# Conditioned low-rank layer and tanh recurrence on one core: the prologue's loads and products in another order, three quarters of W2 in whole rows

## Chip, core and metric

The kernel runs on one NeuronCore of a Trainium2 chip. The metric is the device time of one launch in microseconds (us), the median of the runs shown.

## What is computed

The input x has 4 batches of 512 time steps with 256 channels, all float32. A first layer adds a correction to x. Its weights are partly made from a condition vector per batch:

```
c = layernorm(cond) * gamma + beta
w = gelu(c @ W1 + bias1) @ W2 + bias2          # W2: 256 x 8192
a1, b1, a2, b2 = four parts of w, each 256 x 8 per batch
mid = gelu(x @ base_down + (x @ a2) @ b2^T)
x = x + mid @ base_up^T + (mid @ b1) @ a1^T    # the kernel adds x twice: this sum and the last one
```

A second layer is a recurrence over the 512 steps, `h = tanh(x_t @ Wx + b + h @ Wh)`, and the output is x plus all the h.

## The kernel before

**The stages.** The prologue makes the four factors A2, B2, B1 and A1 from W2, applies them to the first 64 time steps, and prepares the first 16 inputs of the recurrence. Then 512 recurrence steps run one after the other (`over_pairs(recurrence)`, L976). In each step TensorE does 24 small bf16 products on split weights (L881), ScalarE does two tanh (L462), and VectorE makes the residues (L544, L548). Work for later time steps is put between the steps from a table written by hand (`fill_product`, `turn_more_rows` L853, `turn_rows` L864, `input_product`). The order of everything is written out by hand for each engine. Engines meet through semaphores only, and each engine runs its list in order.

**The loads.** SyncE issues all large loads in one list (L307 to L319): the first 64 rows of x per batch, W1, base_down, then A2 and B2 of W2, Wh, base_up, B1, Wx, A1, the other 64 rows of x's first tile, and three more tiles of x. `load_w2` (L301) splits each of the four parts of W2 into four transfers of 128 rows by 1024 columns (4 KB of each row): column half c outside, row half k inside. W2's partition axis holds the rows, k is which 128 of the 256 rows. ScalarE issues six small loads (L393 to L398), the last two being b_rnn and bias2.

**TensorE's list in the prologue** (L651 to L779, L948 to L976): warm-up products on zeros (`keep_busy`, L646 to L649, each a 128x256 bf16 product that nothing reads), the transposed condition (L655), 12 more on zeros, the transposed first rows of x (L669), bias1 (L718), the transposed normalized condition (L722), base_down (L675) and W1 (L732). Then, for each of the four parts, `bias_product` (L661) starts a bank with bias2, and `w_products` (L678) adds, for one column half c, the products of both row halves k. That is 16 instructions on L682: two k, four column strips e, and two passes of a float32 product.

**What VectorE does with them.** `keep_rank` (L521) waits until a column half of a part is complete, multiplies by a mask (L524, wmul) and sums over the rank (L527, fac). `spread` (L530, instruction at L531) lays the factor out as a block matrix, for B2 (b2d) and A1 (a1d) alone. Its list is: A2 halves 0 and 1, a copy, B2 half 0 and its spread, u0 (L558), B2 half 1 and its spread, B1 halves 0 and 1, v0, then for each half n of A1 its rank sum, its spread and `make_x2` (L535). `turn_factor` (L688, instruction at L691) turns A2 and B1 on TensorE. L755 is x @ a2, L767 adds b2d to mid, L698 is base_up, L708 adds a1d, L785 and L790 start the first inputs of the recurrence.

**GpSimd** makes constants, then splits b, Wh and Wx into bf16 parts (L361 to L388). The split of Wh and of Wx takes five instructions each and starts when the load has landed. A memset of h_ring (L389) follows.

Of the kernel before, what the change touches and what calls it, by code (L numbers as in the profile page):

```python
# [32 lines left out]
def adaptive_lowrank_then_recurrence(nc, x, cond, base_up, base_down, ln_gamma, ln_beta, W1, bias1, W2,  # L33
# [24 lines left out]
    with ExitStack() as ctx:  # L58
# [16 lines left out]
        x_sb = sb("x_sb", [P, B, NTT, D])  # L75
# [69 lines left out]
        ld_x = [sem(f"ld_x{n}") for n in range(NTT)]  # L145
        ld_x_more = sem("ld_x_more")
# [84 lines left out]
        def hpre(m):  # L231
            return (bank[7], bank[3])[m][:, D + B * m:D + B * (m + 1)]
# [62 lines left out]
        def _(sp):  # L295
            w2v = W2.rearrange("(k p) (j n) -> k p j n", p=P, j=NTYPE)

            def load_x(n):
                sp.dma_start(x_sb[:, :, n], x[:, P * n:P * (n + 1)].rearrange("b p d -> p b d")).then_inc(ld_x[n], 16)
# [92 lines left out]
        def _(act):  # L392
# [52 lines left out]
            def fill_more_rows(h):  # L445
                act.wait_ge(rows_psum, h + 1)
                nc.scalar.copy(xT[:, :, 2 * h:2 * h + 2, T0:P],
                               more_rows_out(h).rearrange("p (k b t) -> p k b t", k=K2, b=2)).then_inc(rows_moved, 1)
# [40 lines left out]
        def _(dve):  # L489
            steps = [0]  # L490

            def then_wait(ins):
# [23 lines left out]
                                  bank[2][:, 0:K2 * B]).then_inc(cT_ready, 1)  # L516
# [126 lines left out]
        def _(pe):  # L643
            zeros_h = zeros[:].bitcast(BF16)
            pe.wait_ge(pool_step, 1)
            def keep_busy(n, spare=0):  # L646
                for _ in range(n):
                    nc.tensor.matmul(bank[spare][:, D:2 * D], zeros_h[:, 0:P], zeros_h[:, 0:D], start=True, stop=True,  # L648
                                     skip_group_check=True)  # L649

            keep_busy(WARM)  # L651
# [6 lines left out]
            keep_busy(12)  # L658

            def bias_product(j, c):  # L660
                nc.tensor.matmul(wbank(j, c), quadrant[:].rearrange("e i q -> e (i q)"),  # L661
                                 bias2_sb[:, j, c], start=True, stop=False, skip_group_check=True)
# [338 lines left out]
```

## Time and profile before

| | us |
|---|---|
| median of 3 runs (526.58 to 527.30) | 526.85 |
| the profiled execution, device time | 527.65 |
| its span, first to last instruction | 525.9 |
| TensorE busy (matmuls) | 505.6 |
| VectorE busy | 291.8 |
| ScalarE busy | 175.2 |
| GpSimd busy | 22.2 |
| start of the first product of recurrence step 0 after x is ready (L790) | 37.57 |

The profile's times count from the first instruction. PE is TensorE's matmuls and PEld its weight loads, DVE VectorE, ACT ScalarE, POOL GpSimd, SP SyncE, and a q behind an engine means its queue. L682 is line 682 of the kernel. The DMA engines are nearly fully busy in the first 35 us (slices of 13 us move 292, 401 and 213 GB/s) and nearly idle after that. "128x256 f32" is partitions by elements. In the chain that ended last, each piece is followed back from the last instruction to what released it, so its pieces add up to the elapsed time. A piece of PE ends where the next one's result begins, some hundredths of a us after the start that the timeline shows.

### The profile page before, as it was taken

To read this page: it belongs to the slowest core of one execution; us is meant where nothing else is said; L and a number is where in the kernel's file an instruction comes from. 1 tells how busy PE (TensorE), PEld (TensorE's weight loads), DVE (VectorE), ACT (ScalarE), POOL (GpSimd) and SP (SyncE) were. 2 spreads that over 40 slices of the span, in tenths; PEclk is the share of its full clock that TensorE was granted. 3 is DMA by queue.
4 is the path that set the end of the run, shared out by engine and by line. 5 is a ranking of instruction groups with operands and counts; after the bars stand their busy time and mean duration, and the time that the engine had idled before them with its cause. 6 is when DMAs were issued, how large, how long until landed. Compare 5 with 4: busy or idle time off the path is not lost.

```text
span 525.9 us, 33134 instructions
## 1 busy us (share of the span) xinstructions
PE 505.6 (96%) x14756; PEld 471.9 (90%) x14756; DVE 291.8 (55%) x2272; ACT 175.2 (33%) x1158; POOL 22.2 (4%) x35
## 2 busy tenths in 40 slices
PE   9999999999999999999999999999999999998885
PEld 6569999999999999999999999999999999998884
DVE  2535565565556556555655555555655655565553
ACT  3103333333333333333333333333333333333322
POOL 7350000000000000000000000000000000000000
PEclk9999999999999999999999999999999999999999
DMA  8970000000000000000000000000000000000000
GB/s 292 401 213 4 4 14 4 4 14 4 14 5 14 6 7 11 4 14 4 15 4 14 4 6 14 4 14 4 14 4 5 14 4 15 4 14 3 14 6 11
DMA packets 8114, 16.05 MB, mean 31 GB/s; under 512 B 500, under 2 KB 5924, under 8 KB 7972
## 3 DMA queue, kind: packets, MB, share of 16 engines
q1 hardware_dynamic: 7904, 13.90, 7.8%
q8 instruction: 115, 1.88, 1.5%
q14 instruction: 27, 0.22, 0.1%
q10 hardware_dynamic: 68, 0.05, 0.0%
HBM read 11.85 MB, written 2.10 MB: 27 GB/s over the span
## 4 chain that ended last, share of the span: by engine, by line
PE 94%; ACT 3%; issue 1%; DVE 1%; DVEq 0%; POOL 0%; POOLq 0%
PE bank L881 64%; PE bank L801 7%; PE bank L845 4%; PE bank L826 3%; ACT h_ring L462 3%; PE bank L850 2%; PE bank L840 2%; PE bank L821 2%; PE bank L831 2%; PE bank L648 2%; PE bank L682 2%; PE bank L810 1%; PE bank L661 1%; PE bank L785 1%; PE bank L869 1%
## 5 line engine op out<-in xcount | busy, mean ns | idle before, releaser
L881 PE MATMUL bank<-h_ring,whp 128*128 128x52 bf16 x6132 | 243.3, 186 | 13.2 <-ACT h_ring L462 13.2
L544 DVE TENSOR_TENSOR r_ring<-h_ring 128x4 f32<-128x4 f32 x1022 | 136.6, 164 | 205.7 <-ACT h_ring L462 203.2
L462 ACT ACTIVATE h_ring<-bank 128x4 f32<-128x4 f32 x1024 | 142.1, 174 | 320.3 <-PE bank L881 312.5
L881 PE MATMUL bank<-r_ring,whp 128*128 128x52 bf16 x4096 | 220.5, 185 | 0.0
L881 PEld LDWEIGHTS bank<-h_ring,whp 128*128 128x128 bf16 x6132 | 187.9, 96 | 34.2 <-ACT h_ring L462 25.8
L881 PEld LDWEIGHTS bank<-r_ring,whp 128*128 128x128 bf16 x4096 | 174.6, 96 | 0.0
L881 PE MATMUL bank<-l_ring,whp 128*128 128x52 bf16 (+1 forms) x2048 | 157.4, 178 | 0.0
L548 DVE TENSOR_TENSOR l_ring<-r_ring 128x4 bf16<-128x4 f32 x1024 | 136.2, 162 | 0.0
L881 PEld LDWEIGHTS bank<-l_ring,whp 128*128 128x128 bf16 x2048 | 122.5, 96 | 0.0
L801 PE MATMUL bank<-xp,wxp 128*128 128x32 bf16 x1488 | 63.0, 176 | 0.0
L801 PEld LDWEIGHTS bank<-xp,wxp 128*128 128x128 bf16 x1488 | 50.5, 96 | 0.0
L845 PE MATMUL bank<-mid,upT 128*128 128x128 f32 x120 | 28.1, 316 | 0.0
L826 PE MATMUL bank<-xT,down_sb 128*128 128x128 f32 x112 | 26.2, 316 | 0.0
L785 PE MATMUL bank<-ones,b3h 128*128 128x32 bf16 x128 | 22.4, 176 | 0.0
L845 PEld LDWEIGHTS bank<-mid,upT 128*128 128x128 f32 x120 | 17.9, 188 | 0.0
L826 PEld LDWEIGHTS bank<-xT,down_sb 128*128 128x128 f32 x112 | 16.7, 188 | 0.0
L592 DVE TENSOR_TENSOR y_sb<-x2T,h_ring 128x64 f32<-128x64 f32 x64 | 15.4, 283 | 0.6 <-ACT h_ring L462 0.6
L840 PE MATMUL bank<-mid,b1T 128*128 128x128 f32 x60 | 14.0, 316 | 0.0
L850 PE MATMUL bank<-v_sb,a1d 128*128 128x128 f32 x60 | 14.0, 316 | 0.0
L821 PE MATMUL bank<-xT,a2T 128*128 128x128 f32 x56 | 13.1, 316 | 0.0
L831 PE MATMUL bank<-u_sb,b2d 128*128 128x128 f32 x56 | 13.1, 316 | 0.0
L648 PE MATMUL bank<-zeros 128*128 128x256 bf16 x72 | 12.0, 319 | 1.0 <-POOL zeros L338 1.0
(123 smaller groups left out, 240.4 us busy)
## 6 DMA issues: line engine op xcount, KB each, us to landing
w_sb<-in_L_cond_W SPq DMA_DIRECT2D x16, 512.0 KB, 11.5
out<-o_sb SPq DMA_DIRECT2D x16, 128.0 KB
x_sb<-in_x SPq DMA_DIRECT2D x3, 512.0 KB, 15.2
x_sb<-in_x SPq DMA_DIRECT2D x2, 256.0 KB, 9.6
w_sb<-in_L_cond_W SPq DMA_DIRECT2D x1, 256.0 KB, 3.6
down_sb<-in_L_cond_base_down SPq DMA_DIRECT2D x1, 256.0 KB, 5.0
wh_sb<-in_L_cond_Wh SPq DMA_DIRECT2D x1, 256.0 KB, 11.1
up_sb<-in_L_cond_base_up SPq DMA_DIRECT2D x1, 256.0 KB, 11.3
```

The source lines that it names most:

```text
L462: nc.scalar.activation(h_ring[:, m, slot(pair, s), 0:B], zt, ACT.Tanh).then_inc(h_ready, 1)
L544: nc.vector.tensor_tensor(r_ring[:, k, q, 0:B], state_before(pair, s, k)[:, 0:B], state_hi_before(pair, s, k)[:, 0:B], ALU.subtract).then_ ...
L548: nc.vector.tensor_tensor(l_ring[:, k, q, 0:B], r_ring[:, k, q, 0:B], r_hi[:, k, q, 0:B], ALU.subtract).then_inc(l_ready, 1)
L785: nc.tensor.matmul(zbank(p, q, m)[:, 0:TC // 2], b3h[:, P * m:P * (m + 1)], ones[:], start=True, stop=False, skip_group_check=True)
L801: nc.tensor.matmul(zb, wxp[w][:, k, P * m:P * (m + 1)], rhs, start=False, stop=False, skip_group_check=True)
L821: ins = nc.tensor.matmul(columns(fill_out(tile, 0)), a2T[:, k].rearrange("p e q -> p (e q)"), xT[:, k, :, t0:t0 + BL], start=(k == 0), sto ...
L826: nc.tensor.matmul(columns(fill_out(tile, 1 + c)), down_sb[:, k, P * c:P * (c + 1)], xT[:, k, :, t0:t0 + BL], start=(k == 0), stop=False)
L831: nc.tensor.matmul(columns(fill_out(tile, 1 + c)), b2d[:, P * c:P * (c + 1)], u_sb[:], start=False, stop=True).then_inc(fmid_psum, 1)
L840: ins = nc.tensor.matmul(columns(fill_out(tile, 0)), b1T[:, k].rearrange("p e q -> p (e q)"), rhs, start=(k == 0), stop=(k == K2 - 1))
L845: nc.tensor.matmul(columns(fill_out(tile, 1 + c)), upT[:, k, P * c:P * (c + 1)], rhs, start=(k == 0), stop=False)
L850: nc.tensor.matmul(columns(fill_out(tile, 1 + c)), a1d[:, P * c:P * (c + 1)], v_sb[:], start=False, stop=True).then_inc(fup_psum, 1)
L881: return nc.tensor.matmul(zbank(p, q, m)[:, col0:col0 + n], whp[part][:, k, P * m:P * (m + 1)], rhs[:, 0:n], start=False, stop=stop, skip_ ...
```

## The change

- W1 is loaded first and with two adjacent rows per partition (`(p k)` in place of `(k p)`), then base_down and Wh. The condition is turned in the same order. The first rows of x come behind A2, in a tile of their own (xa_sb) with two adjacent time steps per partition. Their transposes are four of 128x128 in place of eight of 64x64. The other 64 rows of the first tile (xb_sb) are loaded and turned the same way. Wx is loaded ahead of B1.
- `load_w2` loads A2, B2 and B1 in two transfers each of 128 whole rows of 8 KB (1 MB), and A1 in four as before.
- On ScalarE bias2 is loaded ahead of b_rnn, and the Gelu of the condition comes ahead of the copies of the turned x.
- On TensorE `w_half_products` does one column half c for one row half k. For A2, B2 and B1 both column halves of k = 0 come first, then both of k = 1, so both halves of a part are complete within one k. All bias products come earlier, into banks that two parts share (B1 and A1 in the upper 256 columns). The x work comes behind A2's products. B1's products come behind base_up, with nine products on zeros behind each k.
- In the last stretch three quarters of A1 come ahead of its first use and one quarter behind it. Some first products of step 0 come earlier.

The diff, cut to its core:

```diff
-        PLACE = {A2: 0, B2: 2, B1: 0, A1: 2}
+        PLACE = {A2: (0, 0), B2: (2, 0), B1: (0, HC), A1: (2, HC)}
         def wbank(j, c):
-            return bank[PLACE[j] + c][:, 0:HC]
+            first, col = PLACE[j]
+            return bank[first + c][:, col:col + HC]
...
             def load_w2(j):
+                if j != A1:
+                    for k in range(K2):
+                        sp.dma_start(w2_sb[:, k, j], w2v[k, :, j]).then_inc(ld_w2[j][0][k], 16)
+                    return
                 for c in range(2):
                     for k in range(K2):
                         sp.dma_start(w2_sb[:, k, j, 2 * CH * c:2 * CH * (c + 1)],
                                      w2v[k, :, j, 2 * CH * c:2 * CH * (c + 1)]).then_inc(ld_w2[j][c][k], 16)
-            sp.dma_start(x_sb[0:T0, :, 0], x[:, 0:T0].rearrange("b p d -> p b d")).then_inc(ld_x[0], 16)
-            sp.dma_start(w1_sb[:], W1.rearrange("(k p) n -> p k n", p=P)).then_inc(ld_w1, 16)
+            sp.dma_start(w1_sb[:], W1.rearrange("(p k) n -> p k n", p=P)).then_inc(ld_w1, 16)
             sp.dma_start(down_sb[:], base_down.rearrange("(k p) n -> p k n", p=P)).then_inc(ld_down, 16)
+            sp.dma_start(wh_sb[:], Wh.rearrange("(k p) n -> p k n", p=P)).then_inc(ld_wh, 16)
             load_w2(A2)
+            sp.dma_start(xa_sb[:].rearrange("p r d -> p (r d)"),
+                         x[:, 0:T0].rearrange("b (q r) d -> b q (r d)", r=2)).then_inc(ld_xa, 16)
             load_w2(B2)
-            sp.dma_start(wh_sb[:], Wh.rearrange("(k p) n -> p k n", p=P)).then_inc(ld_wh, 16)
             sp.dma_start(up_sb[:], base_up.rearrange("(k p) n -> p k n", p=P)).then_inc(ld_up, 16)
+            sp.dma_start(wx_sb[:], Wx.rearrange("(k p) n -> p k n", p=P)).then_inc(ld_wx, 16)
             load_w2(B1)
-            sp.dma_start(wx_sb[:], Wx.rearrange("(k p) n -> p k n", p=P)).then_inc(ld_wx, 16)
             load_w2(A1)
-            sp.dma_start(x_sb[T0:P, :, 0], x[:, T0:P].rearrange("b p d -> p b d")).then_inc(ld_x_more, 16)
+            sp.dma_start(xb_sb[:].rearrange("p r d -> p (r d)"),
+                         x[:, T0:P].rearrange("b (q r) d -> b q (r d)", r=2)).then_inc(ld_xb, 16)
             for n in range(1, NTT):
                 load_x(n)
...
             act.dma_start(bias1_sb[:], bias1.rearrange("(o n) -> o n", o=1)).then_inc(ld_bias1, 16)
+            act.dma_start(bias2_sb[:], bias2.rearrange("(j c e n) -> e j c n", j=NTYPE, c=2, n=HC)).then_inc(ld_bias2, 16)
             act.dma_start(b_rows[:], b_rnn.partition_broadcast(NPART)).then_inc(ld_b, 16)
-            act.dma_start(bias2_sb[:], bias2.rearrange("(j c e n) -> e j c n", j=NTYPE, c=2, n=HC)).then_inc(ld_bias2, 16)
...
-            for k in range(K2):
-                act.wait_ge(tr_ready, k + 1)
-                nc.scalar.copy(xT[:, k, :, 0:T0], bank[6 - k][:, 0:B * T0].rearrange("p (b t) -> p b t", b=B)).then_inc(
-                    tr_moved, 1)
             for m in range(K2):
                 act.wait_ge(hpre_ready, m + 1)
                 nc.scalar.activation(gT[:, m, :], hpre(m), ACT.Gelu).then_inc(g_ready, 1)
+            for k in range(K2):
+                act.wait_ge(tr_ready, k + 1)
+                nc.scalar.copy(xT[:, k, :, 0:T0].rearrange("p b (q r) -> p r b q", r=2),
+                               bank[6 + k][:, 0:B * T0].rearrange("p (r b q) -> p r b q", r=2, b=B)).then_inc(tr_moved, 1)
...
+            def w_half_products(j, c, k):
+                pe.wait_ge(ld_w2[j][c if j == A1 else 0][k], 16)
+                for e in range(NCH):
+                    last = nc.tensor.matmul(wbank(j, c)[Q * e:Q * (e + 1), :], gRep[:, k].rearrange("p b r -> p (b r)"),
+                                            w2_sb[:, k, j, HC * (NCH * c + e):HC * (NCH * c + e + 1)], start=False,
+                                            stop=(k == K2 - 1), skip_group_check=True)
+                if k == K2 - 1:
+                    last.then_inc(w_ready[j], 1)
...
-            pe.wait_ge(ld_x[0], 16)
-            first_transposes(0)
-            first_transposes(1)
-            keep_busy(4)
+            keep_busy(10)
+            pe.wait_ge(ld_bias2, 16)
+            pe.wait_ge(quadrant_ready, 1)
+            bias_product(A2, 0)
+            pe.wait_ge(cn_ready, 1)
+            for k in range(K2):
+                last = nc.tensor.transpose(bank[5][:, D + B * k:D + B * (k + 1)], cn[:].rearrange("b (p k) -> b k p", k=K2)[:, k],
+                                           ident[0:B, 0:B])
+            last.then_inc(cT_psum, 1)
+            bias_product(A2, 1)
+            bias_product(B2, 0)
...
-            pe.wait_ge(cn_ready, 1)
-            for k in range(K2):
-                last = nc.tensor.transpose(bank[2][:, B * k:B * (k + 1)], cn[:, P * k:P * (k + 1)],
-                                           ident[0:B, 0:B])
-            last.then_inc(cT_psum, 1)
-            keep_busy(4)
-            pe.wait_ge(ld_down, 16)
-            base_down_product(0, 0)
             pe.wait_ge(ld_w1, 16)
             pe.wait_ge(cT_ready, 1)
             for m in range(K2):
                     last = nc.tensor.matmul(hpre(m), w1_sb[:, k, P * m:P * (m + 1)], cT[:, k, :], start=False,
                                             stop=(k == K2 - 1), skip_group_check=True)
                 last.then_inc(hpre_ready, 1)
-            base_down_product(0, 1)
-            for k in range(K2):
-                base_down_product(1, k)
-            pe.wait_ge(ld_bias2, 16)
-            pe.wait_ge(quadrant_ready, 1)
-            for c in range(2):
-                bias_product(A2, c)
-            pe.wait_ge(grep_ready, 1)
-            w_products(A2, 0)
-            bias_product(B2, 0)
-            w_products(A2, 1)
             bias_product(B2, 1)
-            keep_busy(4, 7)
-            w_products(B2, 0)
-            pe.wait_ge(fac_ready[A2], 2)
-            turn_factor(A2, a2T_psum)
             for c in range(2):
                 bias_product(B1, c)
+            pe.wait_ge(grep_ready, 1)
+            w_half_products(A2, 0, 0)
+            w_half_products(A2, 1, 0)
+            bias_product(A1, 0)
+            keep_busy(4)
+            w_half_products(A2, 0, 1)
+            w_half_products(A2, 1, 1)
+            pe.wait_ge(ld_xa, 16)
+            first_transposes(0)
+            first_transposes(1)
+            bias_product(A1, 1)
+            pe.wait_ge(ld_down, 16)
+            for m in range(K2):
+                base_down_product(m, 0)
+            pe.wait_ge(fac_ready[A2], 2)
+            pe.wait_ge(tr_moved, K2)
+            turn_factor(A2, a2T_psum)
+            for m in range(K2):
+                base_down_product(m, 1)
+            w_half_products(B2, 0, 0)
+            w_half_products(B2, 1, 0)
             pe.wait_ge(a2T_ready, 2)
             for k in range(K2):
                 last = nc.tensor.matmul(columns(bank[6][:, 0:B * T0]), a2T[:, k].rearrange("p e q -> p (e q)"),
                                         xT[:, k, :, 0:T0], start=(k == 0), stop=(k == K2 - 1))
             last.then_inc(u_psum, 1)
-            w_products(B2, 1)
+            w_half_products(B2, 0, 1)
+            w_half_products(B2, 1, 1)
+            keep_busy(4)
             pe.wait_ge(ld_up, 16)
             for i in range(K2 * K2):
                 last = nc.tensor.transpose(bank[7][:, P * i:P * (i + 1)],
                 nc.tensor.matmul(columns(bank[4 + m][:, 0:B * T0]), b2d[:, P * m:P * (m + 1)], u0_sb[:], start=False,
                                  stop=True, skip_group_check=True).then_inc(mid_psum, 1)
                 keep_busy(4, 6)
-            w_products(B1, 0)
-            for c in range(2):
-                bias_product(A1, c)
             pe.wait_ge(upT_ready, 1)
             for n in range(K2):
                 for k in range(K2):
                     pe.wait_ge(mid_ready, max(n, k) + 1)
                     base_up_product(n, k)
-            w_products(B1, 1)
-            keep_busy(7, 7)
...
                 for k in range(K2):
-                    for b in range(2):
-                        e = 2 * k + b
-                        last = nc.tensor.transpose(more_rows_out(h)[:, T0 * e:T0 * (e + 1)],
-                                                   x_sb[T0:P, 2 * h + b, 0, P * k:P * (k + 1)], ident[T0:P, T0:P])
+                    last = nc.tensor.transpose(more_rows_out(h)[:, P * k:P * (k + 1)], xb_sb[:, h, P * k:P * (k + 1)],
+                                               ident[:])
                 last.then_inc(rows_psum, 1)
...
                     else:
                         for m in range(K2):
                             first_input_product(0, m, 1).then_inc(z_ready, 1)
-                        first_input_product(1, 0, 1)
-                        bias_start(0, 1, 1)
-                        for k in range(K2):
-                            first_input_product(1, 1, k)
+                        for m in range(K2):
+                            first_input_product(1, m, 1)
...
+            w_half_products(B1, 0, 0)
+            w_half_products(B1, 1, 0)
+            keep_busy(9, 6)
+            w_half_products(B1, 0, 1)
+            w_half_products(B1, 1, 1)
+            keep_busy(9, 6)
             pe.wait_ge(fac_ready[B1], 2)
             turn_factor(B1, b1T_psum)
             pe.wait_ge(bp_ready, 1)
             for k in range(K2):
                 v0_product(k)
             w_products(A1, 0)
-            keep_busy(6, 7)
+            w_half_products(A1, 1, 0)
+            keep_busy(7, 7)
             pe.wait_ge(v0_ready, 1)
             pe.wait_ge(a1d_ready, 1)
             a1_first_product(0)
-            w_products(A1, 1)
+            w_half_products(A1, 1, 1)
+            bias_start(0, 1, 0)
             pe.wait_ge(ld_wx, 16)
             pe.wait_ge(x2_first, 1)
             for m in range(K2):
                 first_input_product(0, m, 0)
-            bias_start(0, 1, 0)
             first_input_product(1, 0, 0)
-            keep_busy(8, 7)
+            keep_busy(6, 7)
             pe.wait_ge(a1d_ready, 2)
             a1_first_product(1)
+            bias_start(0, 1, 1)
+            first_input_product(1, 1, 0)
             keep_busy(3, 7)
             pe.wait_ge(x2_first, K2)
             over_pairs(recurrence)
```

## Rows read from the trace of the kernel before

**Rows 1.** The page, the chain that ended last: share of the span by engine.

```profile
PE 94%; ACT 3%; issue 1%; DVE 1%; DVEq 0%; POOL 0%; POOLq 0%
```

**Rows 2.** Waits of TensorE's matmuls, 3 to 38 us: who for whom, us in total, times, longest.

```profile
PE bank L708 <- DVE a1d L531: 0.7, 1, 0.7
PE bank L767 <- DVE b2d L531: 0.3, 1, 0.3
PE bank L691 <- DVE fac L527: 0.2, 1, 0.2
```

**Rows 3.** Two loads: issue (start, us), then KB and us from issue to landing.

```profile
4.29 0.45 SPq L304 DMA_DIRECT2D w_sb<-in_L_cond_W  x1
w_sb<-in_L_cond_W SPq DMA_DIRECT2D x1, 512.0 KB, 7.9
...
15.80 1.33 SPq L304 DMA_DIRECT2D w_sb<-in_L_cond_W  x1
w_sb<-in_L_cond_W SPq DMA_DIRECT2D x1, 512.0 KB, 15.7
```

**Rows 4.** Chain that ended last, 0 to 60 us: start us, us, what.

```profile
0.99 3.59 PE bank L648 x16
...
6.94 0.64 PE bank L669 x8
...
11.95 1.06 PE bank L661 x4
...
14.00 0.62 PE bank L661 x2
...
16.25 0.54 PE bank L648 x4
...
20.35 1.04 PE bank L682 x16
...
21.42 0.44 DVE wmul L524
...
22.33 0.75 DVE b2d L531
...
29.48 0.64 PE bank L691 x16
...
33.84 0.46 PE bank L708 x2
...
37.21 0.33 PE bank L648 x3
...
37.57 0.86 PE bank L790 x6
...
42.62 0.39 PE bank L860 x4
...
50.43 0.28 PE bank L869 x2
```

**Rows 5.** Timeline of VectorE and GpSimd: start us, us, engine, line, operation.

```profile
5.47 0.56 POOL L373 CAST b_part<-b_rows 3x256 bf16<-3x256 f32 x1 [1.16 <-DMA b_rows<-in_L_cond_b]
...
19.19 1.16 POOL L363 TENSOR_TENSOR wres<-wh_sb,whp 128x512 f32<-128x512 f32 x1
...
19.48 1.01 DVE L531 TENSOR_TENSOR b2d<-fac,qmask 128x128 f32<-128x128 f32 x1
...
20.41 0.41 DVE L558 TENSOR_TENSOR u_sb<-bank,bmask 128x256 f32<-128x256 f32 x1
...
22.32 0.61 POOL L366 CAST whp<-wres 128x512 bf16<-128x512 f32 x1
...
25.17 0.62 POOL L362 CAST wxp<-wx_sb 128x512 bf16<-128x512 f32 x1 [2.25 <-DMA wx_sb<-in_L_cond_Wx]
...
29.56 3.94 POOL L389 MEMSET h_ring<- 128x4608 f32 x1
...
33.40 0.29 DVE L531 TENSOR_TENSOR a1d<-fac,qmask 128x128 f32<-128x128 f32 x1
```

More of the change, by code:

```diff
@@ L74, in adaptive_lowrank_then_recurrence @@
         w2_sb = sb("w2_sb", [P, K2, NTYPE, WCOL])
-        x_sb = sb("x_sb", [P, B, NTT, D])
+        xa_sb = sb("xa_sb", [P, 2, D])
+        xb_sb = sb("xb_sb", [P, 2, D])
+        x_sb = sb("x_sb", [P, B, NTT - 1, D])
         up_sb = sb("up_sb", [P, K2, D])
@@ L144, in adaptive_lowrank_then_recurrence @@
         ld_bias2 = sem("ld_bias2")
-        ld_x = [sem(f"ld_x{n}") for n in range(NTT)]
-        ld_x_more = sem("ld_x_more")
+        ld_xa = sem("ld_xa")
+        ld_xb = sem("ld_xb")
+        ld_x = [sem(f"ld_x{n}") for n in range(1, NTT)]
         ld_down = sem("ld_down")
@@ L231, in hpre @@
         def hpre(m):
-            return (bank[7], bank[3])[m][:, D + B * m:D + B * (m + 1)]
+            return bank[7 - m][:, D + B * m:D + B * (m + 1)]
         def slot(pair, s):
@@ L446, in fill_more_rows @@
                 act.wait_ge(rows_psum, h + 1)
-                nc.scalar.copy(xT[:, :, 2 * h:2 * h + 2, T0:P],
-                               more_rows_out(h).rearrange("p (k b t) -> p k b t", k=K2, b=2)).then_inc(rows_moved, 1)
+                nc.scalar.copy(xT[:, :, :, T0:P].rearrange("p k b (q r) -> p r k b q", r=2)[:, h],
+                               more_rows_out(h).rearrange("p (k b q) -> p k b q", k=K2, b=B)).then_inc(rows_moved, 1)
             def fill_rows(tile):
@@ L645, in _, with keep_busy @@
             pe.wait_ge(pool_step, 1)
-            def keep_busy(n, spare=0):
+            def keep_busy(n, spare=4, first=False):
                 for _ in range(n):
-                    nc.tensor.matmul(bank[spare][:, D:2 * D], zeros_h[:, 0:P], zeros_h[:, 0:D], start=True, stop=True,
+                    nc.tensor.matmul(bank[spare][:, D:2 * D], zeros_h[:, 0:P], zeros_h[:, 0:D], start=first, stop=first,
                                      skip_group_check=True)
-            keep_busy(WARM)
+            keep_busy(WARM, first=True)
             pe.wait_ge(const_ready, 4)
@@ L657, in _ @@
             last.then_inc(condT_ready, 1)
-            keep_busy(12)
             def bias_product(j, c):
                 nc.tensor.matmul(wbank(j, c), quadrant[:].rearrange("e i q -> e (i q)"),
-                                 bias2_sb[:, j, c], start=True, stop=False, skip_group_check=True)
+                                 bias2_sb[:, j, c], start=(j in (A2, B2)), stop=False, skip_group_check=True)
             def columns(ps, b=B):
@@ L667, in first_transposes @@
             def first_transposes(k):
-                for b in range(B):
-                    last = nc.tensor.transpose(bank[6 - k][:, T0 * b:T0 * (b + 1)], x_sb[0:T0, b, 0, P * k:P * (k + 1)],
-                                               ident[0:T0, 0:T0])
+                for r in range(2):
+                    last = nc.tensor.transpose(bank[6 + k][:, P * r:P * (r + 1)], xa_sb[:, r, P * k:P * (k + 1)],
+                                               ident[:])
                 last.then_inc(tr_ready, 1)
@@ L676, in base_down_product @@
                                  start=(k == 0), stop=False, skip_group_check=True)
+            def w_half_products(j, c, k):
[6 more added lines that the diff above has]
+                    last.then_inc(w_ready[j], 1)
             def w_products(j, c):
                 for k in range(K2):
-                    pe.wait_ge(ld_w2[j][c][k], 16)
-                    for e in range(NCH):
-                        last = nc.tensor.matmul(wbank(j, c)[Q * e:Q * (e + 1), :],
-                                                gRep[:, k].rearrange("p b r -> p (b r)"),
-                                                w2_sb[:, k, j, HC * (NCH * c + e):HC * (NCH * c + e + 1)], start=False,
-                                                stop=(k == K2 - 1), skip_group_check=True)
-                last.then_inc(w_ready[j], 1)
+                    w_half_products(j, c, k)
             def turn_factor(j, done):
@@ L866, in turn_rows @@
                 if b == 0:
-                    pe.wait_ge(ld_x[n], 16)
+                    pe.wait_ge(ld_x[n - 1], 16)
                 for k in range(K2):
-                    last = nc.tensor.transpose(rows_out(tile)[:, P * k:P * (k + 1)], x_sb[:, b, n, P * k:P * (k + 1)],
+                    last = nc.tensor.transpose(rows_out(tile)[:, P * k:P * (k + 1)], x_sb[:, b, n - 1, P * k:P * (k + 1)],
                                                ident[:])
```

8 lines of the change are left out of this document (5 added, 3 removed).

## The prediction

> **What bounds the kernel now.** I read the chain that ended last first. TensorE has 94% of it [rows 1], and the recurrence, where the change edits almost nothing, starts at 37.57 us (L790) [rows 4]. So the change can move the end only by moving that 37.57, and by what it takes out of the first steps. Next come TensorE's waits between 3 and 38 us. There are three, 0.7, 0.3 and 0.2 us, all on VectorE's factors and none on a load [rows 2]. Third, the landings: the last piece of A2 lands at 4.29 + 7.9 = 12.2 us, the last of A1 at 15.80 + 15.7 = 31.5 us [rows 3]. Loads are behind nobody's wait. TensorE's own list bounds the prologue, and the question is what the new list costs and what VectorE has left to do when it is through.
>
> **Loads, costed at nothing.** A2 has the same 2.75 MB up to its end as before (W1, base_down and Wh in place of x, W1 and base_down), so its end stays near 12.2 us. By the sum below its second row half is wanted at 13.5. From 12.2 to 31.5 us the queue lands 6.75 MB, 0.35 MB per us. That puts x's first rows at 12.9 (wanted at 14.5), B2's end (5 MB) at 18.6 (wanted at 20.1) and Wx (5.5 MB) at 20.1, where GpSimd had waited for it until 25.17 [rows 5]. A1 ends at 31.5 again and its last quarter is wanted at about 35.9. Whole rows may land somewhat sooner or later than half rows: the cover is 1.3 us at A2 and 1.5 at B2, and each us beyond it would cost one. bias2 is new at the head of TensorE's list, wanted at 6.7 where it was wanted at 11.95 [rows 4]; everything of TensorE is queued behind that wait. Its landing is not shown. b_rnn, whose place in ScalarE's queue it takes, had landed by 5.47 us [rows 5]. I take 0, with 0.7 us as the other end. b_rnn itself then lands later, and its user GpSimd has until 30 us.
>
> **TensorE up to B2's second row half.** In the chain this is the difference to 20.35, where B2's last sixteen products start (L682) [rows 4].
> - Products on zeros cost 0.11 each (three in 0.33), four with the switch 0.54 (L648) [rows 4]. Two of the twelve go (0.22), and of three groups of four one stays (1.08). Together -1.30.
> - Four transposes of 128x128 in place of eight of 64x64: 2 x 0.28 in place of 0.64 (L869, L669) [rows 4], -0.08.
> - Bias products: one alone is 0.62, two are 1.06, so each further one is 0.44 (L661) [rows 4]. Before there were groups of 2, 1, 1 and 2 (3.36). Now A1's and B1's are ahead as well, in groups of 1, 2, 3, 1 and 1: 0.62 + 1.06 + 1.50 + 0.62 + 0.62 = 4.42. That is +1.06.
> - base_down is cut in two groups of equal size, a switch more: +0.10, between 0 and 0.2 (0.62 less 0.44 is one).
> - The products with W2 are as many as before.
>
> The start is 20.35 - 1.30 - 0.08 + 1.06 + 0.10 = 20.13 us.
>
> **The tail on VectorE.** Here is the price of taking both column halves of one row half together. Before, B2's column half 0 was complete a turn and two products earlier, and its rank sum and spread were done while TensorE made half 1. Only one rank sum and one spread stood behind 20.35: 21.42 to 23.08. Now both halves end with the second row half, and VectorE's list is unchanged. From 20.13: the first half is ready after two of four strips' worth, 1.07 - 0.50 = 0.57 (21.42 less 20.35, and half of 1.04), so 20.70. Then rank sum 0.91 (21.42 to 22.33), spread 0.75, u0 0.44 (0.41 and a gap), rank sum 0.91, spread 0.52 [rows 4, 5]: 24.23 us, 1.15 later than 23.08.
>
> A spread took 1.01 us while GpSimd did a subtraction, 0.75 while it did a cast, and 0.29 at 33.40, beside the memset that began at 29.56 and took 3.94 [rows 5]. Wx lands at 20.1 now, so its split (three casts of 0.61 and two subtractions of 1.16, 4.15 us in all) lies on 20.2 to 24.4. The first spread starts at 21.6 and is in the middle of it: 0.75. The second starts at 23.7, at its end: the mean of 0.29 and 0.75. Both ends, 0.29 and 1.01, go into the range. The Trainium skill (SBUF — State Buffer, "Who interferes with whom") says that a VectorE instruction with two inputs in SBUF contends with a GpSimd instruction that reads SBUF and not with one that only writes it, and that the later one waits the earlier one out. By that rule the spreads end just behind the GpSimd instruction they meet and an early Wx moves the split on top of B2's spreads, which speaks against this change; the trace agrees in all three spreads above.
>
> **From b2d to B1's turn.** Before, 23.08 to 29.48. A1's two bias products are gone from it (-1.06), nine products on zeros come between B1's row halves (0.54 + 5 x 0.11 = 1.09). B1's first half is ready 0.50 sooner after its last products start, but a second rank sum of 0.91 follows where one had followed. Sum -1.06 + 1.09 - 0.50 + 0.91 = +0.44. The turn of B1 (L691) [rows 4] starts at 31.07, 1.59 late. The other nine zeros lie under the rank sums.
>
> **A1 to the recurrence.** What follows the turn is the same up to the first product with a1d, 33.84 + 1.59 = 35.43; three quarters of A1 lie under VectorE's work there. It takes 0.46, then the last quarter 0.57 to VectorE, rank sum 0.91, spread 0.29, 0.15 to TensorE: 37.81. TensorE's own list (half of 1.04, six first products of some 0.14, six zeros) ends at about the same time. Then 0.22 for the second product with a1d, 0.30 for the bias and product moved here, three zeros 0.33 and 0.07 of switch: 38.73, against 37.57. That is +1.16. Step 0 is shorter by those moved products, 0.30, and its next step was waiting for TensorE alone. The two turns of more rows go from 0.39 to 0.28 each (L860, L869) [rows 4], -0.22. The sum is +1.16 - 0.30 - 0.22 = **+0.64 us**.
>
> The profiled execution took 527.65 us for a span of 525.9; by the sum the changed one takes 528.3. The median of the runs, 526.85, is 0.8 lower, and I move that: **527.5 us**.
>
> **Rivals.**
> - *Faster: TensorE's list is shorter than I count.* It has about ten switches that I cost from neighbours. Every us that TensorE is earlier at B2's second row half passes on to the end, down to B2's landing at 18.6 (-1.5). With spreads of 0.29, if Wx's split falls elsewhere, 0.69 more goes. For a gain over 0.2% the tail must be 1.7 us shorter, b2d ready by 22.5. Time about 525.6. For it: the half products of A1, the zeros and the transposes do go. Against: TensorE had only 1.2 us of waits to give back [rows 2], and bias products merely moved. Chance 0.18.
> - *Slower: GpSimd's split of Wx holds both spreads.* At 1.01 each in place of 0.75 and 0.52 the tail is 0.75 longer: 528.2. It decides from b2d ready at 24.65. For it: the subtraction of 1.16 is the longer half of the split. Chance 0.19.
> - *Slower: the clock.* The first sixteen products on zeros took 3.59 us, 0.22 each, twice the later 0.11 [rows 4]: the lower of the levels of 1.2 and 2.4 GHz, after an idle engine. The new list idles about 0.6 us before u0's product, 0.5 before the second b2d product and 0.6 before B1's turn, against 0.7, 0.3 and 0.2 now [rows 2]. If the clock fell for as long as those 3.59 us, it would cost half of that: 529.3. Chance 0.08. The Trainium skill (TensorE: Matmul & The Clock Gate, "What's actually happening") says that the default is throttled and activity releases it; no row here shows a fall after the first rise.
> - *The whole rows do nothing.* That the packets are no bigger, or are and nothing waits for them, is in my forecast: no load is waited for.
>
> **How the numbers follow.** My forecast, 527.5 with its own range of 526.4 to 528.4, has 0.55. A measurement of this kernel tells about 0.2%, 1.05 us, from no change: 525.8 to 527.9. The forecast's lower edge gives 0.04 to faster, its upper edge (late bias2, slower switches) 0.06 to slower. Faster 0.18 + 0.04 = 0.22; slower 0.19 + 0.08 + 0.06 = 0.33; same 0.45. The range takes in the faster rival and the held spreads: 525.6 to 528.9.
>
> **What would show it.** In the changed profile: no wait of TensorE on a load; B2's second row half at about 20.1 us; VectorE busy without a gap from 20.7 to 24.2 with TensorE waiting for b2d; the turn of B1 near 31.1; the first L790-type product of step 0 near 38.7; the steps themselves as before. It is wrong if bias2 or a W2 load is waited for, if b2d is ready before 23, or if the granted clock falls after its first rise.

## The result, and the profile after

The changed kernel takes **534.02 us** (median of 6 executions, 532.28 to 539.54) where the kernel before takes 526.86 (6 executions, 526.25 to 527.45): a ratio of 1.0146, with a 95% interval of 1.0098 to 1.0194. It is slower by 7.2 us where I forecast 527.5 with a range that ended at 528.9. The profiled execution is the fastest of the six, 532.28 us for a span of 530.5, or 4.6 us over the span of before (525.9). Its mean granted clock is 0.988 and that of the slowest execution 0.978. The kernel before has 0.999 in its profiled execution and 0.996 or more in all 29 that ran beside the experiments below.

The page of the changed kernel gives its span, the clock in forty slices and the chain's shares by engine:

```profile
span 530.5 us, 33121 instructions
PEclk8799999999999999999999999999999999999999
PE 93%; ACT 3%; issue 1%; DMA 1%; DVE 1%; ACTq 0%; DVEq 0%
```

The chain's shares are those of before [rows 1], but the clock shows 8 and 7 tenths in its first two slices of 13.3 us, where the page of before had 9 in all forty. Windows of TensorE's stretches say where. The columns are the stretch, the busy time and number of instructions of PE, PEld, DVE, ACT and POOL, then the granted clock, the DMA share and GB/s. First the changed kernel:

```profile
5.80:9.20 3.40, 2.98 (x21) 2.44 (x19) 1.51 (x6) 0.34 (x3) 0.53 (x2) 1.00 0.93 338
9.20:12.60 3.40, 3.40 (x13) 3.01 (x14) 0.20 (x1) 0.35 (x2) 3.06 (x5) 0.50 1.04 350
12.60:16.00 3.40, 3.40 (x21) 1.36 (x19) 0.00 (x0) 0.00 (x0) 3.14 (x5) 0.50 1.01 260
16.00:19.40 3.40, 3.40 (x23) 1.07 (x21) 0.72 (x2) 0.00 (x0) 3.11 (x5) 0.50 1.05 390
19.40:22.80 3.40, 3.40 (x33) 2.27 (x30) 1.26 (x4) 0.93 (x3) 0.55 (x1) 0.99 1.01 402
```

and the kernel before:

```profile
6.20:9.60 3.40, 3.40 (x32) 2.74 (x31) 0.96 (x5) 0.69 (x3) 3.06 (x5) 1.00 1.00 377
9.60:13.00 3.40, 3.40 (x23) 2.57 (x25) 0.34 (x1) 0.35 (x2) 2.81 (x4) 1.00 1.03 416
```

The clock rose at 5.80 us, fell at 9.21 to the lower of the levels of 1.2 and 2.4 GHz, and rose again at 19.45. Before, it rose once, at 6.17, and stayed up until the recurrence was over. TensorE is busy for all of the three low stretches (3.40 of 3.40 us): it doesn't stay low for want of work. In the stretch ahead of the fall it was busy for 2.98 of 3.40 us; the missing 0.4 is the wait for bias2, which the second experiment takes up.

The chain that ended last, of the changed kernel (start, length, what):

```profile
2.24 4.67 DMA bias_sb<-in_L_cond_bias
6.96 0.69 PE bank L674 x2
7.66 0.12 PE bank L733 x2
7.78 0.97 PE bank L674 x4
8.75 0.34 PE bank L741 x4
9.09 1.65 PE bank L747 x8
10.74 2.85 PE bank L674 x6
13.59 1.86 PE bank L694 x16
15.46 1.15 PE bank L674 x2
16.60 0.97 PE bank L662 x4
17.57 1.87 PE bank L694 x16
19.44 0.61 PE bank L682 x4
20.05 0.62 PE bank L674 x2
...
23.36 1.00 PE bank L694 x16
...
25.43 0.61 PE bank L694 x8
...
28.79 0.68 PE bank L790 x2
...
35.45 0.64 PE bank L707 x16
...
39.81 0.46 PE bank L724 x2
...
43.23 0.86 PE bank L808 x8
```

L674 are the bias products, of 4 rows by 256 columns; L747 are W1's, of 4 columns; L741 is the bias of W1; L662 are the products on zeros, 128 rows by 256; L694 the products with W2. Sixteen products with W2 take 1.86 us here and 1.00 at the higher level, and so on down to 17.57: 1.65 + 2.85 + 1.86 + 1.15 + 0.97 + 1.87 = 10.35 us. At the higher level the same six pieces are 0.99 and 1.49 (rows of the second experiment below, which still had the clock there), then 1.00 and 0.62 (the rows at 23.36 and 20.05), 0.54 [rows 4] and 1.00 again: 5.64. **The fall makes TensorE's list 4.7 us longer.** That isn't what the execution would gain without it. x's first rows landed at 16.96 us, and their transposes (the piece at 19.44) would have been due at 14.7. So about 2.3 of the 4.7 us would have gone into a wait for these rows, which the fall hides, and 2.4 is what the fall alone adds to the 4.6 (an estimate from these rows; the fifth experiment shows the wait itself). Of the other five executions three have lower clocks (0.978, 0.982 and 0.985), so by their means it lasted longer there.

TensorE's waits up to 50 us, in all, times, longest:

```profile
PE bank L662 <- POOL zeros L351: 1.0, 1, 1.0
PE bank L674 <- DMA bias_sb<-in_L_cond_bias: 0.4, 1, 0.4
PE bank L707 <- DVE fac L540: 0.4, 1, 0.4
PE bank L790 <- DVE u_sb L571: 0.2, 1, 0.2
```

The first is the start of the warm-up. The others come to 1.0 us, where before had 1.2 [rows 2]. No load of weights or x is waited for.

### The profile page after: what moved, and what is told of

It reads as the page before. It is cut to its first block, busy times and chain, and to the rows that moved or that the text cites. A ratio compares the mean times of both kernels' runs of the same rounds, so it can differ in the third digit from the quotient of the medians.

```text
span 530.5 us, 33121 instructions
## 1 busy us (share of the span) xinstructions
PE 510.2 (96%) x14752; PEld 473.9 (89%) x14752; DVE 289.7 (55%) x2272; ACT 175.4 (33%) x1158; POOL 21.9 (4%) x35
## 4 chain that ended last, share of the span: by engine, by line
PE 93%; ACT 3%; issue 1%; DMA 1%; DVE 1%; ACTq 0%; DVEq 0%
PE bank L897 63%; PE bank L819 7%; PE bank L863 4%; PE bank L844 3%; ACT h_ring L475 3%; PE bank L868 2%; PE bank L858 2%; PE bank L849 2%; PE bank L839 2%; PE bank L694 2%; PE bank L674 1%; PE bank L828 1%; PE bank L662 1%; DMA bias_sb<-in_L_cond_bias 1%; PE bank L803 1%
## 5 line engine op out<-in xcount | busy, mean ns | idle before, releaser
L662 PE MATMUL bank<-zeros 128*128 128x256 bf16 x76 | 12.7, 320 | 1.0 <-POOL zeros L351 1.0
```

## The experiments

The first question was whether the fall is due to the wait for bias2, to the products that now stand in a row behind it, or to the loads. Each ratio is against the kernel before on the same chip at the same time. The first four share one such (527.27 us, 526.94 to 527.73).

**Wider warm-up.** Twelve more products on zeros, in three places of the changed kernel.

```diff
-            keep_busy(10)
+            keep_busy(14)
...
+            keep_busy(4)
...
+            keep_busy(4)
```

> The changed kernel with 12 more wide products on zeros (128x256) in its head: 14 in place of 10 ahead of the bias2 wait, 4 ahead of bias1, 4 behind W1's products. In the changed kernel the granted clock rose at 5.8 us, fell at 9.2 us and rose again at 19.5 us. Theory 'narrow work': behind 7 us TensorE does almost only products that use 4 of 128 rows or 4 columns, and the clock falls for that. Then wide products between them hold the clock: no second slow stretch, and the time is the sum without the fall, 526.2 us, plus 0.5 to 1.0 for the zeros, so 526.5 to 527.5 us. Theory 'idle': the 0.4 us wait for bias2 is the cause; this kernel covers it too, so the same is expected. Theory 'loads': the clock has nothing to do with the zeros, and the time stays at 532 to 539 us.

Measured: 537.23 us (534.76 to 538.49), ratio 1.0184 (1.0156 to 1.0212). The clock rose at 6.75 and fell at 10.16, for 17.07 us. All four executions have means of 0.981 to 0.984. No wait for bias2 is left in its trace, and TensorE was busy for all of the 3.41 us ahead of the fall. Twelve more zeros didn't keep the clock.

**No idle.** Five narrow products on zeros (4 rows by 256 columns) cover the wait for bias2.

```diff
+                    nc.tensor.matmul(bank[spare][:, D:2 * D], zeros_h[0:NCH, 0:P], zeros_h[0:NCH, 0:D], start=first,
+                                     stop=first, skip_group_check=True)
...
+            keep_narrow(5)
```

> The changed kernel with the wait for bias2 covered by 5 narrow products on zeros (4 rows x 256 columns), nothing else. Theory 'idle': the clock holds and the time falls to about 526.2 to 526.8 us. Theory 'narrow work': the clock still falls near 9 us and the time stays at 532 to 539 us.

Measured: 535.36 us (530.36 to 538.45), ratio 1.0123 (1.0073 to 1.0173). Its chain:

```profile
5.77 0.65 PE bank L667 x5
6.41 0.45 PE bank L679 x2
6.86 0.12 PE bank L739 x2
6.99 0.97 PE bank L679 x4
7.96 0.34 PE bank L747 x4
8.30 0.99 PE bank L753 x8
9.29 1.49 PE bank L679 x6
10.77 1.81 PE bank L699 x16
```

No wait is left ahead of W2's products: TensorE was busy for all of the 6.82 us from the rise at 3.99 to the fall at 10.81. The clock stayed low for 6.83 us, and by their means (0.978 to 0.985) it fell in the other three executions too. The wait isn't needed for a fall; what fills it here is narrow as well. The rows of L753 and of L679 x6 also give the prices at the higher level used above.

**Narrow products in the kernel before.** Two of its groups of four zeros are cut to 4 rows.

```diff
-            keep_busy(4)
+            keep_narrow(4)
...
-            keep_busy(4)
+            keep_narrow(4)
```

> The kernel before with 8 of its wide products on zeros (two groups of 4, at 7.5 and 8.7 us) made narrow (4 rows x 256 columns). They take as long and leave no idle time. Theory 'narrow work': the clock falls in the first 10 us and the time goes up by 3 us or more, 530 to 535 us; if 4-row work at other places alone decides, it could still hold. Theory 'idle': nothing changes, 526.9 us.

Measured: 527.16 and 527.64 us at a mean clock of 0.998, and 536.81 and 536.93 at 0.978; none of the 29 executions of the kernel before is under 0.996. So with eight narrow products in place of wide ones, and no load or order changed, half of the executions take 9.5 us longer at the lower mean. The profiled execution is one of the two in which the clock held, so that the others lost it in the prologue is read from their means alone.

**Half rows.** The changed kernel with A2, B2 and B1 loaded in halves of 4 KB, in the same order.

```diff
-                        sp.dma_start(w2_sb[:, k, j], w2v[k, :, j]).then_inc(ld_w2[j][0][k], 16)
+                        for c in range(2):
+                            sp.dma_start(w2_sb[:, k, j, 2 * CH * c:2 * CH * (c + 1)],
+                                         w2v[k, :, j, 2 * CH * c:2 * CH * (c + 1)]).then_inc(ld_w2[j][c][k], 16)
```

> The changed kernel with A2, B2 and B1 loaded in half rows of 4 KB again (four transfers of 512 KB each, both column halves of one row half first, so the order of use is kept). Theory 'loads' (whole rows cost something): 1 us or more faster than the changed kernel. Theories 'narrow work' and 'idle': the same as the changed kernel, 532 to 539 us with the clock falling near 9 us; without the fall no load was waited for, so at most 0.3 us either way.

Measured: 532.89 us (532.22 to 538.29), ratio 1.0130 (1.0080 to 1.0179), clocks 0.988, 0.988, 0.989 and 0.978: the changed kernel over again. The whole rows aren't the cause. (The other loads stand here as in the changed kernel; the eleventh kernel falls with the loads of before.)

Next the order was undone in the changed kernel. The kernel before took 527.71 us beside these (526.59 to 528.55).

**Bias products late.** They go back to their places of before, and zeros stand where they stood.

```diff
-            bias_product(A2, 1)
-            bias_product(B2, 0)
+            keep_busy(6)
...
-            bias_product(B2, 1)
+            keep_busy(4)
...
+            for c in range(2):
+                bias_product(A1, c)
```

> The changed kernel with the bias products back at the places of the kernel before (A2's behind W1, B2's and B1's between the products with W2, A1's ahead of base_up), and 8 more wide zeros where the head would idle. Theory 'narrow work in one stretch': 8 bias products and W1's behind one another let the clock fall, so here it holds: no slow stretch between 6 and 30 us. By the trace of the changed kernel the time is then 526.2 us plus whatever the loads hold up. Theory 'few engines' (x's first rows are loaded with an outer size of 4, their 128 packets of 2 KB run about 3 at a time, from 10.5 to 16 us, and B2's end lands at 21 us in place of 18.6): with the clock held TensorE waits 1 to 2 us for x's rows and 0 to 1.5 us for B2, so 527.2 to 529 us. If the clock still falls: 532 us or more.

Measured: 533.13 us (532.00 to 537.35), ratio 1.0126 (1.0074 to 1.0178). The clock held in two of four executions (0.998, 0.999; the others 0.982 and 0.991), the profiled one among them. But the time hardly came back: the two executions that held took 532.00 and 532.27 us, where 527.2 to 529 was expected. Its first wait says why:

```profile
PE bank L682 <- DMA xa_sb<-in_x: 2.1, 1, 2.1
```

TensorE at full rate now waits 2.1 us for x's first rows, until 16.24 us, and the fourteen zeros of this kernel all stand ahead of that wait. Windows of this kernel, with the GB/s last:

```profile
12.00:14.00 2.00, 2.00 (x22) 0.87 (x22) 0.22 (x1) 0.00 (x0) 1.82 (x3) 1.00 1.04 253
14.00:16.00 2.00, 0.14 (x4) 0.00 (x0) 1.47 (x4) 0.00 (x0) 1.84 (x4) 1.00 0.99 260
```

The load of x's first rows has the four batches as its slowest dimension. In the changed kernel's trace its 128 packets of 2 KB started from 10.46 to 15.93 us, about 3 at a time, while W1's 128 packets of 2 KB, with the 128 partitions slowest, started from 1.78 to 2.94 us, some 12 at a time. From 12 to 16 us the 8 KB packets of the weights took 499 ns in the median, where 314 is the median of all. The Trainium skill (DMA: Bandwidth & Descriptors, "Why a DMA increments its semaphore by 16 and not by 1") says that a transfer is spread over the largest number of engines up to 16 that divides the slowest dimension of both its sides, which gives 4 here; the trace agrees, with about 3 packets in flight.

**And x by batches.** The same, with each load of x's rows as four transfers.

```diff
-            sp.dma_start(xa_sb[:].rearrange("p r d -> p (r d)"),
-                         x[:, 0:T0].rearrange("b (q r) d -> b q (r d)", r=2)).then_inc(ld_xa, 16)
+            for b in range(B):
+                sp.dma_start(xa_sb[Q * b:Q * (b + 1)].rearrange("p r d -> p (r d)"),
+                             x[b, 0:T0].rearrange("(q r) d -> q (r d)", r=2)).then_inc(ld_xa, 16)
...
```

> As e5_bias_late, and the two loads of x's first tile are issued as four transfers each, one per batch, 32 partitions of 2 KB. Theory 'few engines': the 2 KB packets of x's first rows take under 1.5 us from first to last, B2's end lands near 19 us, TensorE waits for no load, and the time is 1 to 2.5 us below e5_bias_late, 526.0 to 527.0 us, if the clock holds in both. Theory 'loads are hidden anyway': within 0.3 us of e5_bias_late.

Measured: 530.58 us (530.32 to 531.14), ratio 1.0052 (1.0034 to 1.0070), and the clock held in all four (0.996 to 0.998). 526.0 to 527.0 was expected. Two of the same windows:

```profile
12.00:14.00 2.00, 2.00 (x26) 0.93 (x22) 0.00 (x0) 0.00 (x0) 1.84 (x4) 1.00 0.97 324
14.00:16.00 2.00, 2.00 (x23) 1.00 (x15) 1.47 (x4) 0.67 (x2) 1.85 (x3) 1.00 1.00 418
```

B2's end lands 2.5 us sooner, as the issues of its last 1 MB show, the changed kernel's first (issued at 4.93 us, landed 16.8 later) and this one's behind it (issued at 6.29):

```profile
w_sb<-in_L_cond_W SPq DMA_DIRECT2D x1, 1024.0 KB, 16.8
```

```profile
w_sb<-in_L_cond_W SPq DMA_DIRECT2D x1, 1024.0 KB, 12.9
```

Its waits name no load. x's first rows landed at 13.83 us in place of 16.96. Their packets still took from 9.40 to 12.98 us, about 5 at a time, where under 1.5 us was expected: cutting the load shortened it and didn't make it as quick as W1's. What remains over before is the order itself with fourteen zeros more than the change has. The prediction's 528.3 for the profiled execution and 14 x 0.11 for them make 529.8; the profiled execution took 530.72, and these last 0.9 us are not traced.

**Bias products of full height.** bias2 and its left-hand factor are padded to 128 rows with zeros.

```diff
-        bias2_sb = sb("bias2_sb", [NCH, NTYPE, 2, HC])
+        bias2_sb = sb("bias2_sb", [P, NTYPE, 2, HC])
...
-            keep_busy(10)
+            keep_busy(18)
```

> The changed kernel with bias2 and the selection matrix padded with zeros to 128 rows, so that each bias product uses 128 rows in place of 4 (same columns, same duration, same place); 8 more wide zeros cover the later landing of bias2. Theory 'rows used': the 4-row products are what lets the clock fall, so here it holds and the time is 526.5 to 529 us. If W1's 4-column products or something else decides, the clock still falls: 532 us or more.

Measured: 536.03 us (535.42 to 537.03), ratio 1.0156 (1.0138 to 1.0174). It tells nothing of the rows: the padding put off bias2's load, which landed at 11.06 us, TensorE idled for 3.5 us of the 6.83 ahead of the fall at 12.92, and all four means (0.988 to 0.992) show a fall.

**The change's late part alone, in the kernel before.** A quarter of A1's products goes ahead, two first products and a bias are moved, and the x rows behind the first come by batches in one tile and are turned in four transposes.

```diff
-            keep_busy(6, 7)
+            w_half_products(A1, 1, 0)
+            keep_busy(2, 7)
...
-            w_products(A1, 1)
+            w_half_products(A1, 1, 1)
...
```

> The kernel before with only the late part of the change: the third quarter of A1 ahead of its first use, first products of step 0 moved forward, the other 64 rows of x's first tile turned with four 128x128 transposes (loaded as four transfers of one batch). The head is untouched, so the clock holds. By the sum of the prediction: A1's last quarter 0.45, step 0 0.25 to 0.45, the turns 0.27, together 0.9 to 1.2 us faster than before, about 526.2 us beside 527.27. A rival: the pieces lie under other waits, and it is within 0.3 us of before.

Measured: 526.85 us (525.69 to 527.10, 10 executions), ratio 0.9980 (0.9971 to 0.9990). This part is worth 0.9 us.

Beside the last four the kernel before took 527.17 us (526.27 to 527.61).

**Half rows again**, in the kernel whose clock holds. The edit is that of the fourth kernel.

> As e6_late_split (530.6 us, clock held in all four executions, no load waited for), with A2, B2 and B1 in half rows of 4 KB again. It measures the whole rows by themselves. Theory 'whole rows are hidden': within 0.5 us of e6_late_split, and the landings of A2, B2 and B1 within 0.5 us of its. Rival: half rows land the first half sooner and the time falls by 0.5 us or more.

Measured: 530.29 us (529.80 to 530.77), ratio 1.0060 (1.0047 to 1.0074). Against its own before it is 3.1 us over, with whole rows 2.9. Whole rows bring nothing that this can measure.

**Zeros between the bias products.** The change's order, x by batches, and 28 more zeros.

```diff
-            keep_busy(10)
+            keep_busy(14)
...
+            keep_busy(8)
...
+            keep_busy(8)
...
```

> The changed kernel in its own order, with x's first tile loaded per batch (as in e6_late_split) and 28 more wide zeros between the groups of bias products (28 x 0.11 = 3.1 us if none lies under a wait; e1_wide_fill had 12 and the clock fell in all its executions). Theory 'narrow work': enough wide work between them holds the clock, in most executions, and the time is then 527.5 + 2 to 3, so 529 to 531 us. If the clock falls in all of them again, the zeros' share is not what counts, and the time is 535 us or more.

Measured: 540.97, 541.54 and 540.98 us at clocks of 0.982, 0.978 and 0.978, and 531.32 at 0.999. The clock fell at 11.26 us in the profiled execution, which also waited 2.7 us for bias2. TensorE was busy for only 4.10 of the 6.83 us ahead of that fall, so idle time can have had a part in it, and this kernel doesn't tell what zeros between the bias products are worth. One execution without a fall can't carry much, but it has the change's own order with x by batches, and less 28 x 0.11 it is at 528.2, near the prediction.

**The bias products early, in the kernel before.** Nothing else of the change but the shared banks that this needs.

```diff
+            for j in (A2, B2, B1, A1):
+                for c in range(2):
+                    bias_product(j, c)
...
-            for c in range(2):
-                bias_product(A2, c)
...
```

> The kernel before with its loads and its zeros, and all 8 bias products in one stretch ahead of base_down and W1's products (banks as in the changed kernel). The same work, moved. Theory 'narrow work in one stretch': the clock falls near 10 us in most executions and the time is 530 to 538 us. Theory 'loads or x's place': the clock holds, and the time is within 1 us of before, 527 to 528.5 us (the stretch delays the condition's Gelu, which then has to be waited for by up to 1 us).

Measured: 531.10 us (530.19 to 531.21), ratio 1.0071 (1.0055 to 1.0086), clocks 0.987 to 0.993: it fell in all four. Its chain and windows:

```profile
7.96 0.54 PE bank L649 x4
8.50 4.74 PE bank L662 x16
13.24 1.15 PE bank L676 x2
14.40 1.50 PE bank L739 x8
15.90 2.77 PE bank L676 x6
```

```profile
4.10:10.90 6.80, 6.76 (x50) 5.27 (x49) 2.46 (x8) 2.75 (x7) 4.81 (x8) 1.00 1.04 362
10.90:21.10 10.20, 10.20 (x46) 6.75 (x48) 0.66 (x3) 0.35 (x2) 4.26 (x7) 0.50 1.03 399
```

The bias products (L662, two instructions of the profile each here) run from 8.50 without a gap, and the clock falls at 10.9 in the midst of them, TensorE busy for 6.76 of the 6.80 us ahead. This is the fall by itself, with the loads and the zeros of before and no load waited for. The means don't give the time closely: the execution at 0.993 took 531.10 us, no less than those at 0.987 and 0.988.

**A version that beats both.** The late part alone, and the four zeros ahead of B2's first products gone.

```diff
-            keep_busy(4, 7)
```

> As e8_before_tail (526.85 us beside 527.71 for before) without the four zeros ahead of B2's first products. TensorE is the bound there, so 0.4 to 0.54 us faster than e8_before_tail, if the clock holds; the products with W2 around the place are wide. If the clock falls in some executions, those are 3 us or more slower.

Measured: **525.48 us** (524.57 to 526.08, 6 executions), ratio 0.9968 (0.9956 to 0.9979), clocks 0.996 to 0.998. It is 1.7 us under the kernel before, where the late part alone was 0.9 under its own. Its chain at the first b2d and at step 0:

```profile
21.21 1.26 DVE b2d L534
...
36.65 0.86 PE bank L796 x8
```

Step 0 starts at 36.65, where before it was 37.57 [rows 4], although the spread at 21.21 is held by a GpSimd subtraction (21.16 to 22.31) as the prediction's rule would have it.

## Why the prediction was wrong

**The step that failed is the clock**: every term of the sum is taken at the higher level, and the fall stood outside it, as the rival with a chance of 0.08 at 529.3 and as the last of the signs of being wrong. That rival was wrong twice. *Its condition:* I looked only for idle time of TensorE, found gaps of 0.6 us and took the chance from them. The fall doesn't come from idle: it came with every gap filled (second kernel), and in the kernel before with nothing but the bias products moved together (eleventh). What the list does to the clock stood in the diff: six of the eight bias products, of 4 rows, with the bias and W1's products of 4 columns among them, in one stretch just behind the first rise, with the zeros, base_down and x's transposes gone from between them. I costed that stretch by its duration alone, as "bias products merely moved". *Its price:* I took one low stretch of 3.59 us, worth 1.8. It lasted 10.24 us in the profiled execution and made the list 4.7 longer. In the execution of 539.54 us the mean of 0.978 stands for some 21 us at the lower level in the prologue (0.022 x 537.7, doubled, less the 2.4 us that the clock is low at the end of the profiled execution), about 11 us of loss at most, of the 12.7 that it is over before. This is an estimate, and no trace shows that execution.

The Trainium skill (TensorE: Matmul & The Clock Gate, "What's actually happening"), which I had weighed, says that activity releases the throttle; its section "HAM oscillation — how this bites in real kernels" puts the return of the throttle down to gaps in which TensorE idles. The runs here agree with the first if narrow products count for less than wide ones, and differ from the second: the eleventh kernel's clock fell with TensorE busy for 6.76 of 6.80 us.

**Loads at nothing: the second step that failed**, hidden by the first. I had x's first rows at 12.9 us, B2's end at 18.6 and covers of 1.3 to 1.5 us. x's rows landed at 16.96 and B2's end at 21.8, 3.2 late. That nobody waited is luck: TensorE was 5 us late itself. The fifth kernel, where the clock held, paid 2.1 us for it, so without the fall the change would have been slower than forecast as well. The sum by megabytes presumed that every transfer uses all of the queue; this one did not. A2's end came at 13.30 us (12.2 forecast).

**bias2 at 0:** it was 0.4 us, inside the bound of 0.7. That its landing can vary I had not thought of: issued at 2.25 us in the tenth kernel and at 2.24 in the changed one, it landed at 9.11 and at 6.92.

**TensorE's list to B2's second row half:** 20.13 forecast, 25.43 measured; less the 4.7 of the fall, 20.7.

**VectorE's tail:** 4.10 us forecast from there, 3.28 measured. Both spreads took 0.29 (the second at 28.42) and not 0.75 and 0.52:

```profile
25.90 1.16 POOL L378 TENSOR_TENSOR wres<-wres,wxp 128x512 f32<-128x512 f32 x1
27.12 0.61 POOL L379 CAST wxp<-wres 128x512 bf16<-128x512 f32 x1
```

```profile
26.98 0.29 DVE L544 TENSOR_TENSOR b2d<-fac,qmask 128x128 f32<-128x128 f32 x1
```

The tail came so late that the first spread met only the last 0.08 us of the subtraction, and the second a memset. The rule isn't refuted by that, and the twelfth kernel shows a held spread; the forecast's place for the split was off because the tail had moved.

**b2d to B1's turn, and A1 to the recurrence:** from 28.71 to 35.45 it is 6.74 (6.84 forecast), to the first product with a1d 4.36 (4.36), to step 0 3.42 (3.30). These held. The steps got 1.06 us shorter where I had 0.52, half of what came.

**The sum:** step 0 is 5.66 us later than before; less 4.7 that is 0.96, and 1.16 was forecast. So the durations held to a few tenths each. The whole came out at 532.28 where 528.3 stood for the profiled execution, 4.0 over, and at 534.02 in the median where 527.5 stood, 6.5 over. But taking the fall out wouldn't give the forecast back: with 2.3 us of waiting for x's rows the profiled execution would still be some 2.2 us over before (4.6 - 4.7 + 2.3), where +0.64 was forecast. Only the tenth kernel's one execution without a fall, which has x by batches, comes near it.

**The rivals:** the faster one can't be judged, since b2d was never early. GpSimd's hold on the spreads did not occur. "The whole rows do nothing" was right (fourth and ninth kernels).

**Left open:** whether the rows (4 of 128) or W1's columns (4) weigh more, since the seventh kernel spoiled its own test; whether more zeros between the bias products would hold the clock, since the tenth waited for bias2; why the low stretch lasts longer in one execution than in another; and whether in the fifth kernel the wait or the order let the clock fall in two of four executions.

## What to carry to other kernels

When products are moved, read the new list for what TensorE does right after its clock has risen: here narrow products standing together cost more than their durations, though the engine didn't idle. Keep them spread among wide ones where they were, and take the mean granted clock of several executions, since one profile can miss a fall. A delay can also hide a late load, so ask what the next limit would be before a loss is put down to one cause. When a load's slowest dimension is small, cut the load or reorder it, and don't count it by its megabytes.

## What the runs showed of the hardware that I had not expected

- The granted clock fell from the higher level to the lower with TensorE busy throughout: at 10.9 us in the kernel before with its bias products together (busy 6.76 of 6.80 us ahead; four of four executions by their means), and at 10.81 in the second kernel (6.82 of 6.82). With eight products on zeros cut from 128 rows to 4, two of four executions have a mean of 0.978.
- Twelve more wide products on zeros ahead of the narrow ones and between them did not prevent it (four of four executions). The profiled execution had the clock low for 17.07 us, that of the changed kernel for 10.24.
- A load with four batches outermost moved its 256 KB in 5.5 us where W1's 256 KB took 1.2 and the same rows in four transfers 3.6. While it ran the whole queue fell from 412 to 261 GB/s (12 to 14 us, before and after).
